# Layer 1's four experts in pairs with norms tile by tile, gate and routing beside products, and layer 0's last slot group given out by a product

## The reference

```
# layer 0 ffn: 8 experts (512 -> 1024 -> 512) and one shared expert, top 2 per token
x = x + sum over the 2 chosen experts of share_e(token) * swiglu_e(token) + swiglu_shared(token)

# layer 1 ffn: 4 experts, all computed for all tokens, top 2 weighted
scores  = xf @ gate_W + gate_b ;  weights = softmax(top 2 of scores)
expert  = LN(relu(LN(xf @ W1 + b1)*g1 + be1) @ W2 + b2)*g2 + be2
x = x + xf + sum over the chosen e of weights_e * expert_e        # xf = LN(x)
```

## Time and profile before

| | us |
|---|---|
| median of 3 runs | 3698.16 (3697.8 to 3698.46) |
| profiled execution | 3693.97, span 3692.3 |
| TensorE busy | 3166.6 of the span |
| VectorE busy | 1188.0 |
| ScalarE busy | 688.8 |
| all DMA engines, share in layer 0's last groups | 1.01 |

### The profile page before, as it was taken

The page is one execution under the profiler, slowest core; times in us unless marked ns, Lnnn a source line. Parts: engine busy times, 40 slices in busy tenths (PEclk is TensorE's granted clock), DMA queues, the critical chain, the costliest instruction groups (busy, mean ns, idle before and its releaser), DMA issues. The chain is left out here.

```text
span 3692.3 us, 41285 instructions
## 1 busy us (share of the span) xinstructions
PE 3166.6 (86%) x16809; PEld 1544.7 (42%) x16809; DVE 1188.0 (32%) x2465; ACT 688.8 (19%) x1274; POOL 118.4 (3%) x150
## 2 busy tenths in 40 slices
PE   8998889996799799979778989899998897666666
PEld 4444543433344444344446666434445562111111
DVE  3555420001344569754423131203444411000000
ACT  2433101011233231110012121102433111000000
POOL 1000010001000000000000000000000100000000
PEclk9998889998899899989889999899998899777878
DMA  3100079996111021121332121792001237999998
GB/s 140 40 31 35 13 310 421 409 422 241 69 69 45 22 73 63 75 80 46 140 135 103 43 103 53 294 388 86 35 23 45 108 137 324 420 420 420 420 420 365
DMA packets 102711, 654.09 MB, mean 177 GB/s; under 512 B 18850, under 2 KB 28066, under 8 KB 39586
## 3 DMA queue, kind: packets, MB, share of 16 engines
q1 hardware_dynamic: 98402, 638.31, 42.9%
q0 software_dynamic: 4160, 13.63, 1.0%
HBM read 642.40 MB, written 9.50 MB: 177 GB/s over the span
## 5 line engine op out<-in xcount | busy, mean ns | idle before, releaser
L2725 PE MATMUL banks<-ring,h 128*32 128x512 f32 x1024 | 170.9, 784 | 71.0 <-DMA ring<-in_L_ffn_w 47.0
L773 PE MATMUL banks<-wvb,ctxT 128*128 128x512 f32 x512 | 231.0, 596 | 0.0
L2713 PE MATMUL banks<-ring,mine 128*32 128x512 f32 x1024 | 163.1, 701 | 69.2 <-DMA ring<-in_L_ffn_w 67.7
L1634 PE MATMUL banks<-ring,xT 128*64 128x512 f32 x736 | 167.9, 611 | 12.4 <-DMA ring<-in_L_ffn_Wg 5.6
L497 PE MATMUL banks<-normed_features,first 128*128 128x256 f32 x768 | 168.0, 380 | 1.1 <-ACT normed_features L463 1.1
L497 PEld LDWEIGHTS banks<-normed_features,first 128*128 128x128 f32 x768 | 144.7, 190 | 22.9 <-issue 3.2
L2814 DVE COPY mine<-mT 128x32 f32<-128x32 f32 x31 | 5.6, 181 | 449.2 <-PE banks L2713 449.2
L773 PEld LDWEIGHTS banks<-wvb,ctxT 128*128 128x128 f32 x512 | 92.9, 190 | 108.6 <-issue 106.1
L769 PE MATMUL banks<-extraT,wkb 128*128 128x512 f32 x256 | 116.1, 608 | 1.0 <-ACT extraT L879 1.0
L769 PE MATMUL banks<-ctxT,wkb 128*128 128x512 f32 x256 | 115.4, 596 | 1.4 <-PEq L141 1.4
L769 PE MATMUL banks<-ring 128*128 128x512 f32 x256 | 115.4, 596 | 1.4 <-PEq L141 1.4
(11 more groups left out here) (578 smaller groups left out, 4726.6 us busy)
## 6 DMA issues: line engine op xcount, KB each, us to landing
ring<-in_L_ffn_w SPq DMA_DIRECT2D x256, 1024.0 KB, 27.1
ring<-in_L_ffn_Wd SPq DMA_DIRECT2D x24, 2048.0 KB, 23.4
ring<-in_L_ffn_Wg SPq DMA_DIRECT2D x23, 2048.0 KB, 18.2
ring<-in_L_ffn_Wu SPq DMA_DIRECT2D x23, 2048.0 KB, 21.1
wb<-in_L_ffn_W SPq DMA_DIRECT2D x32, 1024.0 KB, 24.5
ctxT<-in_ctxT SPq DMA_DIRECT2D x16, 1024.0 KB, 4.9
first<-in_L_ffn_W SPq DMA_DIRECT2D x16, 1024.0 KB, 19.9
second<-in_L_ffn_W SPq DMA_DIRECT2D x16, 1024.0 KB, 22.0
```

Of the source, the lines that this page charges most:

```text
L773: ins = pe.matmul(ps[:, u % 2, :], ctxT[:, par, k, r * P:(r + 1) * P], wvb[:, k, :], start=(k == 0), stop=(k == C - 1))
L1634: ins = pe.matmul(ps[H * side:H * side + H, 2 * kind + half, :], xT[:, p % 2, k, H * own:H * own + H], rows_of(where[(name, slot)], C)[:, ...
L2713: ins = pe.matmul(ps[B4 * q:B4 * q + B4, 0, :], mine[:, e % 2, k, :], w[:, q * 512:(q + 1) * 512], start=(k == 0), stop=(k == C - 1))
L2725: ins = pe.matmul(ps[B4 * q:B4 * q + B4, 2, :], h[:, Q * n + q, :], w[:, q * D:(q + 1) * D], start=(n == 0), stop=(n == Q - 1))
```

## The change

Layer 0: rows of the last group are no longer stored and fetched. The last 128 rows of `slot_y` are zeroed at the start of the program, so that the indirect loads, which now wait only for groups 0 to 10, fetch zeros for them. A matrix `hots` (one-hot of a token's row in the last group, times its share) is made by eight VectorE instructions, turned by eight small products after group 4 and copied to `hotsT` by ScalarE; after the last group four products of `hotsT` and `o` give the tokens their rows, and four VectorE additions add them. The row index comes from one more product in `rank`.

Layer 1: `gate_scores` and `route` are gone. The gate's products stand in `L1_outputs`, each half after ScalarE has taken it, and their bias is added by VectorE; routing (`choose`) stands at the head of VectorE's part of the expert block. W1 of expert 0 and b1 go into `ring`, which is free after the last filler product, and are asked for there. W1 and W2 have two buffers each. Experts run in pairs (0, 1) and (2, 3), even ones in banks 0 to 3, odd ones in banks 4 to 7. Norms, powers and combination go tile by tile; `add_shift(e)` adds be2 times the token's weight to x, four VectorE instructions, and `choose` does what `route` did in fewer waits.

```diff
+LAST_ROWS = SLOT_ROWS - P
...
+            pool.dma_start(m.slot_y[LAST_ROWS:SLOT_ROWS, :], zero[:]).then_inc(*filled.up(16))
...
# L0_ffn, gpsimd
+                    if p == LAST:
+                        break
                     pool.wait_ge(*o_taken.at(p + 1))
                     pool.dma_start(m.slot_y[p * P:(p + 1) * P, :], o[:, p % 2, :]).then_inc(*stored[p % 2].up(16))
                 for i in range(2):
-                    pool.wait_ge(*stored[i].at(16 * (len(GROUPS) // 2)))
+                    pool.wait_ge(*stored[i].at(16 * ((LAST + 1 - i) // 2)))
...
# L0_ffn, tensor
+                    ins = pe.matmul(ps[:, 5, P:2 * P], full[:], tri[:], start=True, stop=True)
...
+                    if p == OWN_AFTER:
+                        pe.wait_ge(*own_ready.at(1))
+                        for t in range(T):
+                            for i in range(2):
+                                ins = pe.matmul(ps[:, 4, t * P:(t + 1) * P], hots[:, i, t, :], m.ident[:],
+                                                start=(i == 0), stop=(i == 1))
+                        ins.then_inc(*own_turned.up())
+                    if p == LAST:
+                        pe.wait_ge(*o_taken.at(LAST + 1))
+                        for t in range(T):
+                            pe.matmul(ps[:, t, :], hotsT[:, t * P:(t + 1) * P], o[:, LAST % 2, :], start=True, stop=True)\
+                              .then_inc(*last_done.up())
...
# L0_ffn, vector
+                dve.tensor_copy(index[:], ps[:, 5, P:2 * P])
...
+                for t in range(T):
+                    for i in range(2):
+                        ins = dve.tensor_scalar(hots[:, i, t, :], index[:], away[:, i, t:t + 1], share[:, i, t:t + 1],
+                                                ALU.is_equal, ALU.mult)
...
+                for t in range(T):
+                    dve.wait_ge(*last_done.at(t + 1))
+                    dve.tensor_tensor(m.x[:, t, :], ps[:, t, :], m.x[:, t, :], ALU.add)
...
# L1_outputs
-    norm = HalfNorm(m, m.x, m.y, 1e-5, banks=(4, 5, 6, 7))
+    norm = HalfNorm(m, m.x, m.y, 1e-5, banks=(4, 5))
...
+            sp.wait_ge(fill.done.sem, fill.done0 + last)
+            start_loads(sp, expert_loads)
...
+            def gate(half):
+                pe.wait_ge(*norm.taken.at(C * half + C))
+                for t in (2 * half, 2 * half + 1):
+                    for c in range(C):
+                        ins = pe.matmul(ps[:, 7, 4 * t:4 * t + 4], m.yT[:, c, t * P:(t + 1) * P], gw[:, c, :],
+                                        start=(c == 0), stop=(c == C - 1))
+                return ins
...
             norm.turn(pe, 0)
+            pe.wait_ge(gate_sent.sem, gate_sent.made)
+            gate(0)
             norm.turn(pe, 1)
+            gate(1).then_inc(*scored.up())
...
# L1_ffn, sync
+            start_loads(sp, [(hidden_vectors, (g1[:], d["L1_ffn_g1"]), (be1[:], d["L1_ffn_be1"]))])
+            load(w1[1], "L1_ffn_W1", 1, w1_landed[1])
+            start_loads(sp, [(out_vectors, (be2[:], d["L1_ffn_be2"].partition_broadcast(P)),
+                              (b2[:], d["L1_ffn_b2"].partition_broadcast(P)), (g2[:], d["L1_ffn_g2"].partition_broadcast(P)))])
+            for e in range(2):
+                load(w2[:, e], "L1_ffn_W2", e, w2_landed[e])
+            for e in range(2):
+                sp.wait_ge(*first.at(T * e + T))
+                load(w1[e], "L1_ffn_W1", e + 2, w1_landed[e])
+            for e in range(2):
+                sp.wait_ge(*second.at(T * e + T))
+                load(w2[:, e], "L1_ffn_W2", e + 2, w2_landed[e])
...
# L1_ffn, tensor; base(e) = 4 * (e % 2)
+            for e in (0, 2):
+                up(e)
+                up(e + 1)
+                turn_hidden(e)
+                turn_hidden(e + 1)
+                down(e)
+                down(e + 1)
...
# L1_ffn, vector
+            def moments(products, e, t):
+                dve.wait_ge(*products.at(T * e + t + 1))
+                step(dve.bn_stats(m.stats[:, t, :], ps[:, base(e) + t, :]))
+                step(dve.bn_aggr(m.mv[:, t, :], m.stats[:, t, :]))
+                dve.tensor_scalar(m.den[:, t:t + 1], m.mv[:, t, 1:2], 1e-5, None, ALU.add).then_inc(*var_ready.up())
...
+            def norm_hidden(e, n):
+                def scale(t):
+                    dve.wait_ge(*rooted.at(n + t + 1))
+                    return dve.tensor_scalar(h[:, e % 2, t, :], ps[:, base(e) + t, :], m.mv[:, t, 0:1], m.rstd[:, t:t + 1],
+                                             ALU.subtract, ALU.mult)
+
+                for t in range(T):
+                    moments(first, e, t)
+                    if t:
+                        scale(t - 1)
+                scale(T - 1).then_inc(*hidden.up())
...
+            def norm_output(e, n):
+                def scale(t):
+                    dve.wait_ge(*rooted.at(n + t + 1))
+                    dve.tensor_tensor(share[:, t:t + 1], m.rstd[:, t:t + 1], w[:, t, e:e + 1], ALU.mult)
+                    step(dve.scalar_tensor_tensor(part[:, t % 2, :], ps[:, base(e) + t, :], m.mv[:, t, 0:1], g2[:, e, :],
+                                                  ALU.subtract, ALU.mult))
+                    ins = dve.scalar_tensor_tensor(m.x[:, t, :], part[:, t % 2, :], share[:, t:t + 1], m.x[:, t, :],
+                                                   ALU.mult, ALU.add)
+                    return ins
+                for t in range(T):
+                    moments(second, e, t)
+                    if t:
+                        step(scale(t - 1))
+                scale(T - 1).then_inc(*combined.up())
...
+            choose()
...
+            norm_hidden(0, 0)
+            dve.wait_ge(*out_vectors.at(48))
+            add_shift(0)
+            add_shift(1)
+            norm_hidden(1, T)
+            add_shift(2)
+            add_shift(3)
+            norm_output(0, 2 * T)
+            norm_output(1, 3 * T)
+            norm_hidden(2, 4 * T)
+            norm_hidden(3, 5 * T)
+            norm_output(2, 6 * T)
+            norm_output(3, 7 * T)
```

More of the change, by code:

```diff
@@ L1365, in L3_xattn @@
     return oT, w, out_sent
-def gate_scores(m, weights, srcT, E, brow=None, sent=None, ahead=None):
-    scored = m.sig("gate_scored")
-    with m.block() as block:
-        send(block, ahead)
-        @block.tensor
-        def _(pe):
-            pe.wait_ge(sent.sem, sent.made)
-            for t in range(T):
-                for c in range(C):
-                    ins = pe.matmul(m.ps[:, 0, t * E:(t + 1) * E], srcT[:, c, t * P:(t + 1) * P], weights[:, c, :],
-                                    start=(c == 0), stop=(c == C - 1 and brow is None))
-                if brow is not None:
-                    ins = pe.matmul(m.ps[:, 0, t * E:(t + 1) * E], m.ones[0:1, :], brow, start=False, stop=True)
-            ins.then_inc(*scored.up())
@@ L2011, in _ @@
                 for t in range(T):
-                    ins = dve.tensor_tensor(m.x[:, t, :], m.x[:, t, :], m.y[:, t, :], ALU.add)
+                    mine = sc[:, t, :].unsqueeze(2).to_broadcast([P, E, E])
+                    other = sc[:, t, :].unsqueeze(1).to_broadcast([P, E, E])
+                    dve.tensor_tensor(cmp[:, t], other, mine, ALU.is_gt)
+                    ins = dve.tensor_tensor(eq[:, t], other, mine, ALU.is_equal)
                 step(ins)
-                norm(step, first, 0, 0, h, hidden, 0)
@@ L2015, in _ @@
-                with repeat(dve, E - 1) as e:
-                    step = Chain(dve, step_s, e, 7)
-                    norm(step, first, e + 1, 0, h, hidden, 2 * e + 1)
-                    norm(step, second, e, 4, o, normed, 2 * e + 2)
-                    combine(step, e)
-                    step.end()
-                step = Chain(dve, step_s)
-                norm(step, second, E - 1, 4, o, normed, 2 * E - 1)
-                combine(step, E - 1)
+                for t in range(T):
+                    ins = dve.tensor_tensor(eq[:, t], eq[:, t], before[:], ALU.mult)
@@ new lines, in add_shift @@
+            def add_shift(e):
+                for t in range(T):
+                    ins = dve.scalar_tensor_tensor(m.x[:, t, :], be2[:, e, :], w[:, t, e:e + 1], m.x[:, t, :],
+                                                   ALU.mult, ALU.add)
+                step(ins)
+            choose()
+            for t in range(T):
+                ins = dve.tensor_tensor(m.x[:, t, :], m.x[:, t, :], m.y[:, t, :], ALU.add)
+            step(ins)
+            norm_hidden(0, 0)
+            dve.wait_ge(*out_vectors.at(48))
```

271 lines of the change are left out of this document (122 added, 149 removed).

## The result

The changed kernel takes 3650.54 us, the median of four executions run beside the kernel before, which took 3698.29: ratio 0.9864, 95% interval 0.9848 to 0.9879, a gain of 47.8 us. Four executions in another session, with the kernel before beside them again, gave 3648.3 (ratio 0.9869, 0.9854 to 0.9883). The profiled execution is the fastest of its four, 3639.58 us, span 3637.8, so against the profiled one of before the span is 54.5 shorter. The profiled execution is 11 us under the median; what that difference is, is taken up with the experiments.

The account below looks back on a forecast made before the run. TensorE, busy for 86% of the span, was taken as the bound, so its waits and clock count. Gains of 13.6 + 12.3 + 15.6 + 8.3 = 49.8 us turn 3693.97 into 3644.2, plus 4.2 for the median 3648.4; range 3637 to 3660.

Parts of the forecast that it names:

- Layer 0's end: End of layer 0's feed-forward: last group's rows given by products instead of store and fetch, a gain of 13.6 us.
- The delay of the last weights by the fetch: Layer 0's last groups: the early indirect loads take bandwidth from the last weights, costing 1.4 us.
- The 0.4 for the work in front: Before layer 0's first slot group: a small product in `rank` and a 128x128 copy add 0.4 us.
- The seam: Layer 1, from attention outputs to first expert product: gate and routing moved, weights asked for early, a gain of 12.3 us.
- The experts: Layer 1's expert rounds: pairs and norms by tile take 138.4 us instead of 154.0, a gain of 15.6 us.
- the 5.4 us for two cold rounds after the double turns: Layer 1's experts: each even expert's down round, after turn, wait, turn, loses 2.7 us of clock, twice.
- The tail: End of layer 1's expert stage: last product to last VectorE addition takes 4.6 us instead of 12.9, gain 8.3.
- After the stage: Layer 2 onward: its first instruction follows 0.5 us later in both kernels, and nothing behind it changes.
- clock holds: Rival: TensorE stays at 2.4 GHz over the seam and double turns, 9.8 us less, 3638.6; chance 0.20.
- Fetch ahead of the weights: Rival, layer 0's end: the fetch is served first, delaying weights 4.9 to 7.1 us, about 3653; chance 0.20.
- VectorE the bound: Rival, layer 1's down rounds: GpSimd's power and VectorE's scaling block each other, 2.6 us more, 3651; chance 0.07.
- Slower: Rival, layer 1's experts: denser rounds get 1.2 GHz for long, 15 us more per round, up to 3761; chance 0.03.

Follow-up runs that it names:

- the half alone: Only layer 0's part of the change against the kernel before, layer 1 left as before: 3685.38 us, ratio 0.9969.
- experiment 6: Changed kernel, but GpSimd asks for the eight fetches of finished rows only when the last group's hidden rows are turned: 3649.03 us, ratio 0.9872.
- experiment 3: Changed kernel, but the first expert's up weights and bias rows are asked for at the expert stage's start: 3652.99 us, ratio 0.9877.
- experiment 5: The kernel with all four tiles' norms at once, but the even expert's 16 transposes given three times over: 3653.54 us, ratio 0.9881.
- experiment 4: Changed kernel, but one power for all four tiles of a norm, with the scaling behind it: 3661.33 us, ratio 0.991.
- experiment 2: Stage lengths compared across traces, and the changed kernel with one or two small loads added at the very start: medians 3647.76 and 3650.54 us.

## Why the prediction came out right

The time was forecast at 3648.4 and is 3650.54 and 3648.3; the mechanism is the one named. By its steps:

- **Layer 0's end**, 13.6 forecast: 13.0 by time in the half alone; in the traces the stage is 15.1 shorter in the profiled execution and 10.1 to 13.2 in the ten others with the early fetch. The 5.0 for the new chain fit: 875.48 to 880.59 is 5.1. The last down product at 868.4 is 0.6 to 2.6 earlier than said, because the group's first product began 2.4 us ahead of before (845.83 against 848.21). The delay of the last weights by the fetch was **mis-sized**: 1.4 said, 2.4 measured (experiment 6), and the sum had nothing for the clock that is lost in the longer wait, 1.6 to 2.8 us in ten of eleven traces. The 0.4 for the work in front was not there: the first slot group's tokens are turned 62.5 us after the stage's first load, and 62.7 before the change. So this term came close partly by luck. The size of the delay was worked out from 262 KB in 8.3 us, 32 GB/s, but most of these 8.3 us are no transfer: the store is issued at 846.36, and the DMA view of before shows its packets moving from about 850 to 853, 74 of them with 0.26 MB, 87 GB/s, beside 74 packets of weights. The fetch moves at the same rate, 0.82 MB in the 10 us from 856 (82 GB/s), and 0.82 MB at 428 GB/s are 1.9 of the 2.4 us. The Trainium skill, "DMA: Bandwidth & Descriptors", section "Queues, rings and completion order", says that an engine takes a packet from each queue in turn; by the profile's packets the trace agrees, 226 against 240. What the prediction added to it, turns of equal bytes, did not hold: a packet of the weights has 14.7 KB on average here and one of the fetch 3.4.
- **The seam**, 12.3 forecast: 12.85. The gate's second half took 3.58 at half clock (3.7 said), and no landing is on the path, because the weights are asked for early; without that it would be 5.7 (experiment 3).
- **The experts**, 15.6 forecast: 22.3 (131.67 against 153.95). This is the step that **failed**: the 5.4 us for two cold rounds after the double turns were not there, in any of nine traces with tile-wise norms in pairs (eighteen double turns). The waits are 0.92 each and not 1.15: a power of one column takes 0.54 on GpSimd and not 1.01, and the rest of the chain some 0.2 more than said. The size was read from the earlier trace rows, where a turn and a wait stand together, and taken for both. 7.41 us of transposes alone keep the clock (experiment 5), 3.54 us of standing still in between lose it (experiment 4). The Trainium skill, "TensorE: Matmul & The Clock Gate", section "Part 4: PE-mode transpose", says that transposes don't count as work; for these, float32 and 128x128, the traces don't agree. By these two kernels, what the earlier trace rows showed as the price of a turn and a wait was the price of the wait.
- **The tail**, 8.3 forecast: 8.6 (4.26 against 12.83).
- **After the stage** nothing was to change; by the span's end 4 of the 58.5 us were given back, 2.1 in layer 2's cross attention and 2.0 in layer 3's last part. The second is a stage whose length differs between executions; the first is longer in every trace with layer 1's change, by 1.5 to 6.7 us (experiment 2), a cost that the sum had put at nothing. It hid part of the surplus of the experts: the sum was 4.6 short of the gain of the profiled execution (54.4) and 2.0 over the gain of the medians. That the forecast is this close is partly errors that cancel.

The rivals: *clock holds* was right for the double turns (5.4 of its 9.8) and wrong for the seam and the first round, where the gate and the first bias product (2.09) ran at half clock. *Fetch ahead of the weights* is out by 2.4 against 4.9 and more. *VectorE the bound*: a scaling from the banks takes 0.75 beside a power by GpSimd (1741.02) and 0.74 where GpSimd rests (1742.67), so these two don't block each other. *Slower*: the granted clock is 1.00 over 1645 to 1740.

## What to carry to other kernels

Two units in turn, each with its own banks, give a norm time beside the other's products; cut the norm by tiles too, since what is left of it after the last product is what TensorE stands for (0.92 against 3.54 us) and the clock was lost in the longer standing, at a price above that of the wait (5.2 us more of waiting, 7.7 of clock). A rest that must be (turning) is cheap if TensorE is the one that works in it. When a fetch is moved beside a stream of weights, take its rate from the stretch in which its packets move (87 GB/s for one store, 82 for eight fetches), not from bytes over the time to landing (32), and count the clock that TensorE loses in the longer wait.

## What the runs showed of the hardware

- Transposes of 128x128 in float32 hold TensorE's clock at 2.4 GHz for 7.4 us (64 in a row, granted clock of 1640 to 1665: 1.00), the same at both double turns. The gate's products of 4 columns are another case: its first half, after 0.96 us of waiting, took 1.92 us at the full clock, and its second, after a turn in which the clock had already fallen (1.75 us for 1.04) and 0.75 us of waiting, 3.58 at half (granted 0.50); whether the small products or the waits between lowered the clock is not settled, no run here separates them. Behind the first tile of a product they took 1.84 again (1612.39).
- GpSimd's power takes 0.54 us for 128x1 and 1.01 us for 128x4.
- GpSimd's queue and the queue of the weights, both with work, moved about as many packets each (74 and 74 from 850 to 853 before; 240 and 226 from 856 to 866 after), of 3.4 to 3.5 KB against 13 to 15. So GpSimd's queue got 82 to 87 GB/s, with one request or with eight, and eight fetches of 256 KB delayed the last weights by 2.3 to 2.5 us.
- Beside the full stream of weights GpSimd's requests moved their first packets some 4 us after their issue (846.36 to 850.0 or a little later; 851.67 to 855.5 or later); on idle engines within 2 (876.38 to 877.0, 879.47 to 881.0, by the DMA view in steps of half a microsecond).
- Executions of one kernel lie up to 13 us apart with the change and 15 before it (0.4% both), built up from stages that come out 2 to 4 us apart; a gain of 5 us has to be read in the trace.
